# Activations transposed by DMA, and the first group's W2 moved behind tile 6

## What is computed

```python
def layernorm(x): m, v = mean(x), var(x); return (x - m) / sqrt(v + 1e-5)

# layer 1: a gated linear recurrence over time
u = x @ W_in.T                         # 1024 -> 256
gates = silu(x @ W_sel_in.T) @ W_sel_out.T   # a, b, c, d, 256 each
h_t = sigmoid(a_t) * h_{t-1} + tanh(b_t) * u_t
y = (tanh(c) * h + d_param * sigmoid(d) * u) @ W_out.T

# layer 2: the FFN
act_quant(x)    = round(127 / max|x over features| * x) / scale     # one scale for a token
weight_quant(w) = clip(round(w / mean|w|), -1, 1) * mean|w|         # -1, 0, 1
h = act_quant(x) @ weight_quant(w1).T          # 1024 -> 4096
h = silu(depthwise_conv1d(h, conv_w, conv_b))  # three taps along time, padding 1
y = act_quant(h) @ weight_quant(w2).T          # 4096 -> 1024
```

## Time and profile before

| | us |
|---|---|
| runs (3), median | 1315.16 (1313.01 to 1318.36) |
| profiled execution | 1316.7 |
| its span on the slowest core (core 5) | 1315.2, granted clock 0.950 |
| spans of the other cores | 1308.8 to 1314.9 |

### The profile page before, as it was taken

How to read it: one execution, slowest core, us unless ns; L and a number is a source line. 1 busy time by engine, 2 the same in 40 slices (tenths; PEclk the granted TensorE clock), 3 DMA queues, 4 the chain that set the end, 5 groups by cost and what they waited for, 6 DMA issues and landing times.

```text
span 1315.2 us, 18619 instructions; the slowest of 8 cores (1308.8 to 1315.2 us)
## 1 busy us (share of the span) xinstructions
PE 1168.4 (89%) x6184; PEld 603.1 (46%) x6184; DVE 1106.9 (84%) x2302; ACT 855.1 (65%) x1131; POOL 419.2 (32%) x654
## 2 busy tenths in 40 slices
...
GB/s 206 319 331 218 186 256 292 311 310 185 207 198 44 46 39 75 49 48 50 80 49 65 49 49 49 54 76 48 65 49 49 49 51 47 33 33 33 63 67 33
DMA packets 40099, 146.51 MB, mean 111 GB/s; under 512 B 4804, under 2 KB 4804, under 8 KB 39748
## 3 DMA queue, kind: packets, MB, share of 16 engines
q1 hardware_dynamic: 39572, 142.69, 33.8%
...
...
HBM read 114.36 MB, written 33.55 MB: 112 GB/s over the span
## 4 chain that ended last, share of the span: by engine, by line
PE 69%; DVE 16%; ACT 5%; DMA 4%; SPq 2%; issue 2%; POOL 1%; POOLq 0%; DVEq 0%; ACTq 0%
PE pF L850 32%; PE pO L721 27%; DMA stg<-w1T 4%; PE pF L326 4%; SPq L72 2%; DVE h L760 2%; PE pO L372 2%; DVE xs L393 1%; DVE h L765 1%; DVE hsc L356 1%; PE pF L953 1%; DVE h L753 1%; PE pT L447 1%; DVE accP L780 1%; DVE ysb L361 1%
## 5 line engine op out<-in xcount | busy, mean ns | idle before, releaser
L850 PE MATMUL pF<-w2q,h 128*128 128x512 fp8e4 x2048 | 480.1, 380 | 1.8 <-DVE h L839 1.8
L721 PE MATMUL pO<-xqT,w1q 128*128 128x512 bf16 x1792 | 427.1, 382 | 5.6 <-ACT xqT L452 5.6
L850 PEld LDWEIGHTS pF<-w2q,h 128*128 128x128 bf16 x2048 | 200.6, 98 | 241.8 <-issue 4.6
L727 ACT ACTIVATE hp<-pO 128x512 bf16<-128x512 f32 x224 | 133.6, 596 | 218.8 <-PE pO L721 217.4
L721 PEld LDWEIGHTS pO<-xqT,w1q 128*128 128x128 fp8e4 x1792 | 175.2, 98 | 213.8 <-issue 10.8
L760 DVE SCALAR_TENSOR_TENSOR h<-hp,cwt,h 128x512 bf16<-128x512 bf16 x256 | 202.8, 792 | 0.7
L746 ACT ACTIVATE bt<-hp,cwt 128x512 bf16<-128x512 bf16 x256 | 183.9, 718 | 6.1
L772 ACT ACTIVATE h<-h 128x1024 bf16<-128x1024 bf16 x128 | 134.9, 1054 | 76.1 <-DVE h L765 75.7
L833 DVE TENSOR_TENSOR h<-h,bc 128x512 bf16<-128x512 bf16 x256 | 151.0, 590 | 0.0
L896 POOL TENSOR_SCALAR sm<-sm 128x1 f32<-128x1 f32 (+1 forms) x33 | 17.2, 522 | 376.6 <-DVE sm L883 376.6
L765 DVE TENSOR_TENSOR h<-h,bt 128x512 bf16<-128x512 bf16 x256 | 115.6, 452 | 14.7 <-ACT bt L746 1.3
...
## 6 DMA issues: line engine op xcount, KB each, us to landing
stg<-w1T SPq DMA_DIRECT2D x40, 512.0 KB, 15.3
xs<-x SPq DMA_DIRECT2D x32, 512.0 KB, 11.2
stg<-w2T SPq DMA_DIRECT2D x32, 512.0 KB, 9.1
x2c<-xs SPq DMA_DIRECT2D x32, 512.0 KB, 9.0
stgC<-w2T SPq DMA_DIRECT2D x32, 512.0 KB, 5.9
x2r<-x2c SPq DMA_DIRECT2D x31, 512.0 KB, 4.6
out<-yev SPq DMA_DIRECT2D x31, 512.0 KB, 3.0
x2q<-x2c SPq DMA_DIRECT2D x28, 512.0 KB, 3.3
```

Source lines behind the costliest of these rows:

```text
L721: p_w1[n] = P(lambda e, k=k: e.matmul(bankW1(n), w1q[:, HD * k + 128 * c:HD * k + 128 * (c + 1)], xT[:, :, k, :], start=(k == 0), stop=(k ...
L727: a_ev[n] = A(lambda e: e.activation(hp3[:, n % 8, 2:514], bankW1(n), AF.Identity), *((v_stt[n - 8], a_bt[n - 8], g_sv[n // 4 - 2]) if n > ...
L850: p_w2[m] = P(lambda e, c=c, jj=jj: e.matmul(pb[:, 512 * jj:512 * (jj + 1)], h43[:, ring(32 * f + c), 128 * g:128 * (g + 1)], w2q[:, D * c ...
```

## The change

- `turn_x` takes the place of `quant_T` and `quant_Tev` in the FFN loop, for the groups 4 to 31: one transposing DMA from `xqmB` into `xqT`, issued by SP in step r = 5 behind the load of r = 4. `quant_x` of the next group waits for it, since it rewrites `xqmB`. The transposes of the first four groups stay on TensorE.
- `quant_rnd` writes the rounded hidden values of group 0 into a tile of their own, `held`, and W2 of group 0 isn't run in the steps 38 to 45. W2 slots count on to NW + 8; slot 28 (`HELD`) is group 0, and groups 28 to 31 take the slots 29 to 32, eight steps later than before.
- The last token's hidden values are written to column 0 of `held` (row 0 of group 0), with its scale in row 0 of the scale column. `last_mm` and the separate end for one row go. `last_hidden` is cut into four parts, behind the steps 256 to 259. The held group is loaded and stored in three pieces (row 0, 112 rows, 15 rows).
- `x2r` has one buffer, loaded after the previous group's addition; its memset goes.
- `fin_end`: the last group is scaled, added (now by VectorE) and stored in two halves of 512 columns.

```diff
-    def dma(self, en, out, in_, sem, *toks):
+    def dma(self, en, out, in_, sem, *toks, turn=False):
         self.wait(en, *toks, (sem, self.cnt.get(sem, 0)))
         self.cnt[sem] = self.cnt.get(sem, 0) + 16
-        self.q[en].append(lambda e, S: e.dma_start(out=out, in_=in_).then_inc(S[sem], 16))
+        kind = {"transpose": True} if turn else {}
+        self.q[en].append(lambda e, S: e.dma_start(out=out, in_=in_, **kind).then_inc(S[sem], 16))
         return (sem, self.cnt[sem])
...
-    hxq = sb("hxq", 32, BF16)
+    held = sb("held", 32 * 128, BF16)
     yev = [sb("yev%d" % k, D, F32) for k in range(2)]
-    x2r = [sb("x2r%d" % k, D, F32) for k in range(2)]
+    x2r = sb("x2r", D, F32)
...
+        def turn_x(gi, dst, xqm, *toks):
+
+            p_t2[gi] = a_t2[gi] = q.dma("sy", dst.rearrange("p (k t) -> p k t", k=8), xqm[:, :],
+                                        "tx", v_xq[gi], *toks, turn=True)
...
         def quant_rnd(m):
-            v_q[m] = V(lambda e: e.tensor_scalar(piece(m), piece(m), RC, -RC, OP.add, OP.add),
+            dst = held3[:, 4 * m:4 * m + 4, :] if m < 8 else piece(m)
+            v_q[m] = V(lambda e: e.tensor_scalar(dst, piece(m), RC, -RC, OP.add, OP.add),
                        q_tok[m])
 
+
+
+        HELD = NG - 4
+
+        def group(Gx):
+            return Gx if Gx < HELD else Gx - 1
+
         def w2_mm(m):
-            f, g, j = m // 32, (m % 32) // 8, m % 8
-            Gx = m // 8
+            Gx, j = m // 8, m % 8
+            f, g = group(Gx) // 4, group(Gx) % 4
             pb = pairW2[Gx % 2]
-            q.wait("t", v_q[m], *(v_w2q[4 * j:4 * j + 4] if m < 8 else ()),
-                   a_fa[Gx - 2] if Gx >= 2 and j == 0 else None)
+            q.wait("t", v_hxq[0] if Gx == HELD else v_q[8 * group(Gx) + j],
+                   *(v_w2q[4 * j:4 * j + 4] if Gx == 1 else ()),
+                   a_fa[Gx - 2] if Gx >= 3 and j == 0 else None)
             for c in range(4 * j, 4 * j + 4):
+                hid = (held3[:, c, :] if Gx == HELD else
+                       h43[:, ring(32 * f + c), 128 * g:128 * (g + 1)])
                 for jj in range(2):
-                    p_w2[m] = P(lambda e, c=c, jj=jj: e.matmul(
-                        pb[:, 512 * jj:512 * (jj + 1)],
-                        h43[:, ring(32 * f + c), 128 * g:128 * (g + 1)],
+                    p_w2[m] = P(lambda e, c=c, jj=jj, hid=hid: e.matmul(
+                        pb[:, 512 * jj:512 * (jj + 1)], hid,
                         w2q[:, D * c + 512 * jj:D * c + 512 * (jj + 1)],
                         start=(c == 0), stop=(c == 31)), inc=(c == 4 * j + 3 and jj == 1))
 
         def rows(Gx):
 
-            if Gx == 0:
-                return 1, 128, 0
-            if Gx == NG:
-                return 0, 1, T_TOK - 1
-            return 0, 128, 128 * Gx - 1
+            if Gx == HELD:
+                return [(0, 1, T_TOK - 1), (1, 113, 0), (113, 128, 112)]
+            return [(0, 128, 128 * group(Gx) - 1)]
 
...
         def load_x2(Gx):
             if Gx > NG:
                 return
-            p0, p1, r0 = rows(Gx)
-            x2_ld[Gx] = q.dma("sy", x2r[Gx % 2][p0:p1, 0:D], x2_h[r0:r0 + p1 - p0, :],
-                              "x2l%d" % (Gx % 2), g_fo[Gx - 2] if Gx >= 2 else fin_ready[0],
-                              v_x2z[0])
+            x2_ld[Gx] = [q.dma("sy", x2r[p0:p1, 0:D], x2_h[r0:r0 + p1 - p0, :],
+                               "x2l%d" % k, g_fo[Gx - 1] if Gx >= 2 else fin_ready[0])
+                         for k, (p0, p1, r0) in enumerate(rows(Gx))]
 
...
         def fin_store(Gx):
-            p0, p1, r0 = rows(Gx)
-            d_out[Gx] = q.dma("sy", out_h[r0:r0 + p1 - p0, :], yev[Gx % 2][p0:p1, :],
-                              "ot%d" % (Gx % 2), g_fo[Gx])
-
-
-        p_last, v_lastg, v_hxq = [None], [None], [None]
+            d_out[Gx] = [q.dma("sy", out_h[r0:r0 + p1 - p0, :], yev[Gx % 2][p0:p1, :],
+                               "ot%d" % (Gx % 2), g_fo[Gx]) for p0, p1, r0 in rows(Gx)]
+
+        def fin_end():
+
+            Gx, k = NG, NG % 2
+            pb, Y, X2 = pairW2[k], yev[k], x2r
+            toks = []
+            for n in range(2):
+                h = slice(512 * n, 512 * (n + 1))
+                toks.append(A(lambda e, h=h: e.activation(
+                    Y[:, h], pb[:, h], AF.Identity, bias=sc("bF", k), scale=sc("rF", k)),
+                    *d_out[Gx - 2], g_fc[Gx]))
+            for n in range(2):
+                h = slice(512 * n, 512 * (n + 1))
+                t = V(lambda e, h=h: e.tensor_tensor(Y[:, h], Y[:, h], X2[:, h], OP.add),
+                      *x2_ld[Gx], toks[n])
+                for p0, p1, r0 in rows(Gx):
+                    q.dma("sy", out_h[r0:r0 + p1 - p0, h], Y[p0:p1, h], "oe%d" % n, t)
+
+
+        v_lastg, v_hxq = [None], [None]
+
+        def hold_scale():
+            v_lastg[0] = V(lambda e: e.tensor_copy(sc("g2x"), cols4("g2", 0)[:, 0:1]), v_g2[0])
...
             t0 = A(lambda e: e.activation(X0, X0, AF.Silu), t0)
+            yield
             mc = sc("mxx")
             t1 = V(lambda e: e.tensor_reduce(mc, X0, AX, OP.max, apply_absolute_value=True), t0)
-            t1 = P(lambda e: e.matmul(pT0[0:1, 0:128], mc, identf[:, :], start=True, stop=True),
-                   t1, v_sc[NF - 1])
+            t1 = P(lambda e: e.matmul(pT1[0:1, 0:128], mc, identf[:, :], start=True, stop=True),
+                   t1, pT1_free[0])
+            yield
             m1, i1, s1, g1 = [sc(n)[0:1, :] for n in ("mabx", "invx", "scx", "g2x")]
-            t1 = V(lambda e: e.tensor_reduce(m1, pT0[0:1, 0:128], AX, OP.max), t1)
+            t1 = V(lambda e: e.tensor_reduce(m1, pT1[0:1, 0:128], AX, OP.max), t1)
             t1 = V(lambda e: e.tensor_scalar(m1, m1, 1e-5, None, OP.max), t1)
             t2 = V(lambda e: e.reciprocal(i1, m1), t1)
             v_lastg[0] = V(lambda e: e.tensor_scalar(g1, m1, wcons[0:1, 2:3], 1.0 / 127.0,
-                                                     OP.mult, OP.mult))
+                                                     OP.mult, OP.mult), v_lastg[0])
             t2 = V(lambda e: e.tensor_scalar(s1, i1, 127.0, None, OP.mult), t2)
-            t2 = P(lambda e: e.matmul(pT1[:, 0:1], ones[0:1, :], s1, start=True, stop=True),
-                   t2, v_bc2[NF - 1])
-            t2 = V(lambda e: e.tensor_copy(mc, pT1[:, 0:1]), t2)
+            t2 = P(lambda e: e.matmul(pT1[:, 0:1], ones[0:1, :], s1, start=True, stop=True), t2)
+            yield
+            pT1_free[0] = t2 = V(lambda e: e.tensor_copy(mc, pT1[:, 0:1]), t2)
             t2 = V(lambda e: e.tensor_scalar(X0, X0, mc, RC, OP.mult, OP.add), t2)
-            v_hxq[0] = V(lambda e: e.tensor_scalar(hxq[:, :], X0, -RC, None, OP.add), t2)
-
-        def last_mm():
-            pb = pairW2[NG % 2]
-            q.wait("t", v_hxq[0], a_fa[NG - 2])
-            for c in range(32):
-                for jj in range(2):
-                    p_last[0] = P(lambda e, c=c, jj=jj: e.matmul(
-                        pb[0:1, 512 * jj:512 * (jj + 1)], hxq[:, c:c + 1],
-                        w2q[:, D * c + 512 * jj:D * c + 512 * (jj + 1)],
-                        start=(c == 0), stop=(c == 31)), inc=(c == 31 and jj == 1))
-
-        fin_ready, v_x2z = [None], [None]
+            v_hxq[0] = V(lambda e: e.tensor_scalar(held3[:, :, 0], X0, -RC, None, OP.add), t2, v_q[7])
+            yield
+
+        fin_ready, last = [None], last_hidden()
...
-            if 0 <= m < NW:
+            if 8 <= m < NW + 8:
                 w2_mm(m)
-            if m == NW:
-                last_mm()
...
                 if r == 5:
-                    quant_T(gq, xqmB, pT1b, pT1_free)
-                if r == 6:
-                    quant_Tev(gq, xqT[gq // 4 % 2][:, D * (gq % 4):D * (gq % 4 + 1)], pT1b, pT1_free,
-                              *((p_w1[32 * (gq // 4 - 2) + 31],) if gq >= 8 else d_x2[NG - 2:NG]))
+                    turn_x(gq, xqT[gq // 4 % 2][:, D * (gq % 4):D * (gq % 4 + 1)], xqmB,
+                           *((p_w1[32 * (gq // 4 - 2) + 31],) if gq >= 8 else d_x2[NG - 2:NG]))
 
             cv = n - 1 if 0 <= n - 1 < NW else None
...
                 scales(f1 - 1)
+                if f1 == 1:
+                    hold_scale()
             next(work, None)
             if n == 31:
                 q.wait("v", v_w2q[31], *kw_free, *d_x2[NG - 5:NG])
                 q.wait("sy", *done_a, v_x2[NG - 1], p_o[NG - 1])
-                v_x2z[0] = V(lambda e: e.memset(x2r[0][0:1, :], 0.0))
             if n == 32:
-                for Gx in range(2):
-                    load_x2(Gx)
+                load_x2(1)
 
             if n < NW and n % 4 == 3:
                 save(n // 4)
 
-            if m >= 8 and m % 8 == 0 and m // 8 - 1 < NG:
+            if m >= 16 and m % 8 == 0 and m // 8 - 1 < NG:
                 fin_stats(m // 8 - 1)
                 fin_chain(m // 8 - 1)
-            if m >= 10 and m % 8 == 2 and (m - 10) // 8 < NG:
```

(12 more changed lines are left out.)

50 lines of the change are left out of this document (19 added, 31 removed).

## The result

| | before | after |
|---|---|---|
| median of the runs (4 and 4), us | 1314.2 | 1301.09 (1300.38 to 1301.51) |
| profiled execution, us | 1316.7 | 1301.36 |
| its span on the slowest core, us | 1315.2 (core 5) | 1299.7 (core 0) |
| spans of the other cores, us | 1308.8 to 1314.9 | 1291.7 to 1296.7 |

The ratio is 0.9891, 95% interval [0.9873, 0.9908]. Forecast were 1298.4 us, 16.8 us less; the range and the sign held. In some runs of most kernels the cores of a die are slower at a lower clock: the medians count these runs too, the ratios and the profiles don't.

What follows compares the result with a forecast made beforehand. TensorE was taken to set the FFN's pace, VectorE some 6% behind. Terms 1.5 + 5.0 + 8.0 + 1.5 + 0.8 = 16.8 us less took the 1315.2 us span to 1298.4, range 1291 to 1309.

Steps and rivals of the forecast that it cites:

- Steady tiles: Tiles 2 to 6: transposes leave TensorE, VectorE can follow; 1.6 us a tile, 8.0 us less, between 4.0 and 9.0.
- rival (c): Whole kernel: the engines give way to each other fully; 23.0 us less, 1292 us; chance 0.09.
- Rival (a): Whole kernel: VectorE takes the place as bound at once; only 9.9 us less, 1305.3 us; chance 0.17.
- The transfer: Transposing DMA on SP behind the x2q load: lands in 5 us, costs nothing up to 11 us in steady tiles.
- The upper bound of 11.5 us: Transfer's longest time: 1,024 pieces of 256 B at the queue's mean 0.18 us each, 64 per engine.
- Up to the first meeting: Stretch until 433 us, VectorE the bound: evictions removed from ScalarE give 1.5 us less, from 0 to 3.
- the removed memset only lengthens that same wait: Before the first meeting: removing VectorE's x2r memset only lengthens its wait for hp eviction and centring; no gain.
- the 0.9 for the last eviction: Before the first meeting: the 1.01 us eviction at 418.23, ahead of the hp eviction, goes; 0.9 us gained.
- three more such evictions in tile 0 may give 0.2 each: Tile 0: three further ScalarE evictions removed may give 0.2 us each.
- Tile 1: From 433 to the meeting at 545, group 0's W2 held back: gain is what VectorE saves, 5.0 us, 3.5 to 6.5.
- Tail: Spreading last_hidden over four steps gives 1.5 us, from 0 to 3; the held group's place covers no wait.
- The end: Last scaling, addition and store in halves: 1.6 us less before a longer store; net 0.8 us, 0 to 1.5.

Runs made afterwards that it cites:

- e5: Changed kernel with the eight TensorE transposes of each group run as well, result unread, without ScalarE's eviction; 1310.7 us, ratio 0.9952.
- e6: Changed kernel with each transposing transfer issued three times in a row to the same place; 1307.5 us, ratio 0.9929.
- e7: Changed kernel with each transposing transfer issued eight times in a row to the same place; 1511.5 us, ratio 1.1491.
- e1: Kernel before with only the transposing transfers in place of transposes and evictions of groups 4 to 31; 1306.4 us, ratio 0.9917.
- e12: Changed kernel with groups 4 to 7 transposed on TensorE and evicted on ScalarE as before, transfers from group 8 on; 1293.4 us, ratio 0.9847.
- e10: Changed kernel with TensorE transposes and ScalarE eviction, unread, run beside the transfers for groups 4 to 7; 1294.7 us, ratio 0.9855.
- e2: Changed kernel with transposes on TensorE and evictions on ScalarE as before, the other edits kept; 1307.7 us, ratio 0.9935.
- e8: Changed kernel with the held group's 64 W2 matmuls also run in their old place in tile 1, result unread; 1303.2 us, ratio 0.99.
- e9: Changed kernel with last_hidden in one piece behind step 258 and the last group added and stored whole; 1300.4 us.
- e4: Changed kernel with the held group placed behind the last tile's four groups instead of ahead; 1305.5 us, ratio 0.9912.
- e11: Changed kernel run once more, unaltered, on another chip; 1296.5 us, ratio 0.9871.

## Why the prediction was right, point by point

Measured on core 0, 16.3 us less from the first W1 to the end, against a sum of 16.8. The terms:

- **Steady tiles: 8.9, forecast 8.0.** The mechanism is shown by e5, and VectorE gave way fully: TensorE's 9.0 us, rival (c)'s figure for this term, not the 1.6 a tile that I took. How it gave way was not as said. Only the 0.8 us of waits for hp went; the waits for the centring, which I had counted as 2.2 us that it can give, rose to 4.4. What fell was its busy time, from 107.20 to 104.13 us from meeting to meeting (tile 2, core 0) with the same instructions, since two of its accN no longer lie beside GpSimd's centring (1.52 us each before, 0.68 after) and the scalings (L840) beside GpSimd's additions take 1.4 us less. Rival (a) is out; the meeting's wait stayed 0.61. Periods of 112.6 were forecast and came.
- **The transfer: forecast 5 us to landing with 11 us of room; 4.5, and e6 and e7 put the room at 11.1 without a loss, and at 26.3 less 16.7 and 28.2 less 17.0.** The upper bound of 11.5 us was far off: by the estimate above a piece of 256 B costs 0.025 us, not the queue's mean of 0.18. From the 1309 ns that the Trainium skill, page "VectorE: DVE Perf Modes", section "The three transpose paths", gives for one 128x128 tile, the estimate for eight in a row was 10.5 us; the 4.5 measured, and 3.1 with no load ahead, speak against adding up its single figure.
- **Up to the first meeting: 0.8 us more, forecast 1.5 less. This term failed, in three steps.** The first is "the removed memset only lengthens that same wait", which put the memset at nothing: its going took that wait away and gave 1.2 us (120.17 in e1, 119.00 after). The second is the 0.9 for the last eviction: it isn't on the path, and from the last `quant_x` to the meeting it is 19.60 us without it (after) and with it (e12). The third is "three more such evictions in tile 0 may give 0.2 each": leaving ScalarE's eviction out moved the engines against each other so that VectorE met GpSimd's fp32 work twice for once. e10 puts this at 1.9 us (119.00 against 117.07). I had costed a removed instruction by its length on a stretch where three engines wait for one another in turn. TensorE waits 5.24 us for the transfer where it had waited 5.64 for the eviction.
- **Tile 1: 5.2, forecast 5.0.** The held half alone gives 5.05 (e2), and there the parts are near those forecast: VectorE's busy time falls from 105.65 to 102.28 us, 3.4 where 1.45 + 2.1 were taken, and its idle time by 1.7 where 1.3 were. With the transfers its busy time falls to 99.53, but its idle time rises by 2.6, and the tile is as long. That the gain is only what VectorE saves goes too far: TensorE's 13.8 us, put back, cost 3.0 (e8). TensorE was idle 9.7 us of tile 1, and its clock stood at 0.97 there, where it had been 0.98.
- **Tail: 2.5 (1.2 in the last period, 1.3 up to the statistics), forecast 1.5**; e9 gives 2.2 for the spreading of `last_hidden`. The place of the held group is worth nothing (e4), as said.
- **The end: from the statistics to the end of the span 9.1 us before and 8.6 after, 0.5, forecast 0.8.** Two halves are worth 2.15 us (e9), but before a single row had to be stored.
- **The sum.** That 16.3 came for 16.8 is in part luck: the first stretch was 2.3 us below its term and the end 0.3, and the steady tiles (0.9), the tail (1.0) and tile 1 (0.2) were above theirs.

The remaining 1.3 us between 1298.4 and the span of 1299.7 are mostly not the FFN's: its first W1 came at 315.83 us on the slowest core, where it had been 314.77. And the median fell by 13.1 us, not 16.8: the profiled execution before, 1316.7, lay 2.5 us above the median of 1314.2 of that kernel's runs, while the one after lay at its median. In e11, on another chip, the same kernel was 17.2 us below the kernel before. A forecast made against one profiled execution carries 2 to 3 us of this scatter.
